# Layer 0 of a two-layer graph network: gathered sums in steps 1 to 19 of each body in place of 0 to 20

## The reference

```python
h = relu(layernorm(x));  deg = segment_sum(1, dst) + 1;  dis = rsqrt(deg)
g = (h @ W) * dis
agg = segment_sum(g[src], dst) * dis + (h @ W) * dis * dis
x = x + h + gelu(agg + b)
```

## Time and profile before

| | before |
|---|---|
| median of the runs | 3957.04 us |
| profiled execution | 3974.8 us, span 3973.0 us |
| mean granted TensorE clock | 0.769 |
| busy PE, VectorE, ScalarE, POOL | 70%, 41%, 33%, 37% of the span |
| loop of layer 0 | from 186.4 to 1191.7 us |

### The profile page before, as it was taken

The page is one execution under the profiler, slowest core; times in us unless marked ns, Lnnn a source line. Parts: engine busy times, 40 slices in busy tenths (PEclk is TensorE's granted clock), DMA queues, the critical chain, the costliest instruction groups (busy, mean ns, idle before and its releaser), DMA issues.

```text
span 3973.0 us, 102120 instructions
## 1 busy us (share of the span) xinstructions
PE 2800.8 (70%) x37635; PEld 2380.6 (60%) x37635; DVE 1621.9 (41%) x4904; ACT 1292.0 (33%) x3188; POOL 1478.0 (37%) x1462
## 2 busy tenths in 40 slices
PE   2457777677784777777777777777777777777778
PEld 2335555555563666666666666666666666666666
DVE  8735544444556333333333333333333333333333
ACT  0135555454563222222222222222222222222222
POOL 0654444333424334333333333333333333333331
PEclk6668888787886777877777777777777777777778
DMA  1000000000002122112211121221122112112211
GB/s 44 19 18 16 16 16 16 15 15 15 16 10 52 40 40 42 39 38 41 40 39 41 39 40 39 41 40 39 38 42 40 39 39 42 39 38 42 39 39 38
DMA packets 365051, 133.31 MB, mean 34 GB/s; under 512 B 312657, under 2 KB 342455, under 8 KB 364919
## 3 DMA queue, kind: packets, MB, share of 16 engines
q1 hardware_dynamic: 320248, 85.81, 9.9%
q0 software_dynamic: 44672, 45.83, 6.5%
HBM read 123.94 MB, written 7.54 MB: 33 GB/s over the span
## 4 chain that ended last, share of the span: by engine, by line
PE 67%; issue 23%; DVE 5%; another core or an unknown queue 4%; ACT 1%; DVEq 0%; POOL 0%; DMA 0%; PEldq 0%; ACTq 0%; SPq 0%; POOLq 0%
PE psum L1662 13%; PE psum L1651 12%; PE psum L1717 11%; PE psum L1519 7%; PE psum L1551 7%; PE psum L1641 7%; PE psum L1675 3%; PE psum L1699 3%; PE psum L1540 2%; PE psum L1530 1%; ACT hT L1286 1%; DVE Z L957 1%; PE psum L1485 0%; DVE work L834 0%
## 5 line engine op out<-in xcount | busy, mean ns | idle before, releaser
L673 POOL DMA_INDIRECT rows<-a_rows,idx x980 | 973.2, 993 | 1717.8 <-DMA idx<-src_by_tile 1432.9
L1651 PE MATMUL psum<-wb,eoT 128*64 128x64 f32 x6272 | 502.9, 267 | 461.4 <-issue 451.7
L1651 PEld LDWEIGHTS psum<-wb,eoT 128*64 128x64 f32 x6272 | 371.8, 170 | 571.5 <-issue 569.8
L1286 ACT ACTIVATE hT<-psum 128x392 bf16<-128x392 f32 x1152 | 518.8, 503 | 500.6 <-PE psum L1551 285.6
L1662 PE MATMUL psum<-Y,Z 128*128 128x64 bf16 x8820 | 526.4, 235 | 162.5 <-issue 162.4
L673 POOL DMA_INDIRECT rows<-g_rows,idx x416 | 411.7, 990 | 550.4 <-DMA idx<-src_by_tile 430.7
L1551 PE MATMUL psum<-Z,lo_hi 128*128 128x392 f16 x1152 | 419.5, 380 | 259.7 <-issue 169.7
L1662 PEld LDWEIGHTS psum<-Y,Z 128*128 128x128 bf16 x8820 | 465.2, 126 | 219.3 <-issue 200.2
L1519 PE MATMUL psum<-work,hT 128*128 128x192 bf16 x3528 | 513.6, 269 | 15.9 <-issue 13.2
L1356 ACT ACTIVATE Y<-psum 128x512 f16<-128x512 f32 (+1 forms) x392 | 150.0, 435 | 1151.1 <-PE psum L1699 1147.7
L1374 ACT ACTIVATE Y<-psum 128x384 bf16<-128x384 f32 (+1 forms) x588 | 255.6, 439 | 769.6 <-remote 580.9
(11 more groups left out here) (273 smaller groups left out, 2344.7 us busy)
## 6 DMA issues: line engine op xcount, KB each, us to landing
work<-in_edge_attr_dram SPq DMA_DIRECT2D x392, 128.0 KB
Z<-slot_code SPq DMA_DIRECT2D x196, 96.0 KB
rows<-a_rows,idx POOLq DMA_INDIRECT x980
rows<-g_rows,idx POOLq DMA_INDIRECT x416
idx<-src_by_tile SPq DMA_DIRECT2D x197, 2.5 KB, 1.7
wb<-b_rows SPq DMA_DIRECT2D x196, 16.0 KB
g_rows<-Y SPq DMA_DIRECT2D x1, 1600.0 KB, 7.1
a_rows<-Y SPq DMA_DIRECT2D x6, 256.0 KB, 2.3
```

The source lines that it names most:

```text
L673: pool.indirect_dma_start(out=rows[:, k, t, :], out_offset=None, in_=table, in_offset=bass.IndirectOffsetOnAxis(ap=idx[:, k, t:t + 1], axis=0)
L1286: nc.scalar.activation(counts[:, j % 2, :, t * SLOTS:(t + 1) * SLOTS], psum[:, t % 4, 0:KEYS].rearrange("p (h m) -> p h m", m=SLOTS), ACT.Copy
L1651: TT.matmul(psum[half:half + D, 2 + k % 2, t * D:(t + 1) * D], eoT[:, k % 2, t, half:half + D], wb[:, k, :], start=(t == 0), stop=False)
```

## The change

`order_of_adds` takes its places from another rule; `gathered_at` goes.

```diff
-        def gathered_at(j, steps, count):
-            q = -(-j * count // steps)
-            return q if -(-(j + 1) * count // steps) > q else None
-
         def order_of_adds(steps, count):
-            at = [gathered_at(j, steps, count) for j in range(steps)]
+            when = {1 + q * (steps - 2) // count: q for q in range(count)}
+            at = [when.get(j) for j in range(steps)]
             place_gathered, place_counted, n = [], [], 0
```

## The result

The changed kernel takes 3936.21 us (median of 20 runs, 3924.57 to 3948.18); the kernel before, in 20 runs taken with them, 3948.56 us (3932.97 to 3960.59). Forecast were 3954 us, no change, and a range of 3943 to 3973. Two things are in the miss: the 3 runs that the forecast started from had a median of 3957.04, 8.5 us above that of the 20; and the change brought 10.7 us where 2.9 were forecast.

The account below looks back on a forecast made before the run. Layer-0 gather bursts on POOL were taken to stall PE's tiles on the way to ACT for nearly their own length. Start -6.7, rows of four +3.8, rest 0: -2.9 us, from 3957.04 to 3954, range 3943 to 3973.

Parts of the forecast that it names:

- part 2: Order inside layer-0 bodies: rows of four sums cost +3.8 us, ends -4 and +7.6.
- a dearer third burst: Looped bodies: the third burst in a row of three costs 8.6 us, 1.0 more than the first two.
- Part 1: Start of body 0: step 0 without a sum, PE goes on with step 1; net -6.7 us, ends -10.2 and -3.5.
- the signs that I had named: Layer-0 start: rows wait under 2 us, first sum at 235 to 242, burst 4 alone; wrong if before 210 or after 246.
- the branch I named in one sentence: Body 0's start: PE finishes step 1 and its sum before the stall, burst 4 joins the run; gain 8.45 us.
- my sign for the looped bodies: The two looped bodies at 311 to 318 us each; wrong above 325 or below 305.
- Part 3: Last body: sums 48 to 51 in steps 1 to 4; 0 us, ends +-1.
- What a burst costs: Layer-0 gather bursts on POOL: 7.87 us each in the looped stretch, 6.5 us each in body 0.
- Rival B: Layer 0: bursts cost PE nothing, only the 10.4 us wait for first rows goes; 3946.6 us; chance 0.12.
- Rival A: Rows of four decide: each fourth burst meets the third's undrained stall; slower, 3973 to 3984 us; chance 0.17.
- Rival C: Start pays to -10.2 and rows of four cost nothing, or free steps pay -4; 3943 to 3947 us; chance 0.19.

Follow-up runs that it names:

- loops only, 5: Kernel before with the looped and last bodies as changed, body 0 as before, on chip 5: 3975.45 us, 0.9997 of the kernel before.
- start only, 5: Kernel before with only body 0's first three sums moved to steps 1, 2, 3, on chip 5: 3971.15 against 3977.15 us, 0.9990.
- body 0 only, 9: Kernel before with only body 0 as changed (rows of four from step 1), on chip 9: 3929.74 us, 0.9973 of the kernel before.
- row of 16, 5: Changed kernel with the looped bodies' sixteen sums in steps 1 to 16, on chip 5: 3963.94 us, 0.9960 of the kernel before.
- first sum in 2: Changed kernel with body 0's first sums in steps 2 to 6: chip 5 3958.36 us, 0.9947; chip 9 3924.52 us, 0.9953 of the kernel before.
- experiment 5: Kernel before with seven of eight gathers of each layer-0 burst left out: chip 9 3540.47 against 3941.30 us, 0.8982; chip 2 0.9925, also in new order.

## Why the prediction was wrong, point by point

Two terms were mis-sized. The base was 3957.04 us where 20 runs give 3948.56. And part 2, the rows of four, stood in the sum at +3.8 us and measured -1.2 (-5 to +3); its cause, a dearer third burst, came of pricing a step without a sum like one with a sum. Part 1 came near in size, but by a path that did not happen. With the measured terms the sum is 3948.6 - 8.9 - 1.2 = 3938.5; 3936.21 came, 3937.9 by the ratio.

Stretches of the layer-0 loop read from the traces (from the first tile matmul of one step to that of another), us:

| kernel, chip | steps 0 to 3 | steps 4 to 21 | sum | bodies 1, 2 |
|---|---|---|---|---|
| before | 90.4 | 237.5 | 327.9 | 629.2 |
| loops only, 5 | 93.0 | 240.1 | 333.1 | 625.0 |
| start only, 5 | 79.6 | 243.1 | 322.7 | 623.7 |
| body 0 only, 9 | 76.0 | 240.6 | 316.6 | 602.0 |
| changed | 78.6 | 240.2 | 318.8 | 605.9 |
| changed, 9 | 78.0 | 245.7 | 323.7 | 597.5 |
| row of 16, 5 | 76.6 | 249.5 | 326.1 | 609.4 |
| first sum in 2, 5 | 66.9 | 250.6 | 317.5 | 625.1 |
| first sum in 2, 9 | 65.9 | 248.0 | 313.9 | 609.8 |

**Part 1, the start: near in size by luck, wrong in the path.** Forecast -6.7 (-10.2 to -3.5). Two traces with the old start end body 0 at 330.5 on average, five with the first sum in step 1 at 321.6: -8.9, with a scatter of up to 9.5 us inside the five, four of which have the new order in body 0 too. The timed run of the start alone says -4 (-9 to +1). But I had PE caught by the stall after five or six tiles of step 1, at 0.8 us a tile, and burst 4 left alone. In fact all sixteen tiles got through at 0.4 us each before the stall began, PE waited 6.0 us for rows, and burst 4 joined the run as before (a gather every 1.25 us until 241.59). Three of the signs that I had named are answered by it: the first sum came at 204 us, before the 210 that I had called a sign of being wrong; the wait for rows was not under 2 us; and burst 4 stood behind no gap. That is the branch I named in one sentence at 8.45 us, one whole step. The step that failed is the tile's price, taken from the stretch's mean clock and not from the tiles of step 0, which stood in the earlier trace rows at 0.4 us.

**Part 2, the rows of four: wrong.** Forecast +3.8 (0 to +7.6 in its reasoning), measured -1.2 (-5 to +3). On chip 5 the looped bodies took 623.7 us in the old order and 625.0 and 625.1 in the new; on chip 9 602.0 against 597.5 and 609.8. There is no difference beyond their scatter, which also takes in my sign for the looped bodies (303 us each in the changed kernel's first trace, under the 305 that I had called wrong, and 299 to 313 in the four others with rows of four). The error can be redone from my own rows: I priced every step at 8.45 us with or without sum. With 7.21 and 1.24 (experiment 5) a pair is 40.6 - 3 x 7.21 - 2 x 1.24 = 16.5, 8.2 a burst, and a row of three 57.65 - 4 x 7.21 - 3 x 1.24 = 25.1, 8.4 a burst. The dearer third burst was the free step counted too high. The earlier trace rows gave the price of a step with a sum, and the sentence that the sum is within that figure was right; that a step without one costs the same was not looked up. The last row spoke against it: its five steps took 41.2 us, less than 5 x 8.45 = 42.25.

**Part 3, the last body: right**, 48.5 us in both traces.

**What a burst costs: right, with some luck.** 7.87 us forecast from one trace, 7.7 (7.4 to 8.0) when the gathers were taken away. With 7.21 for a step and 1.24 for a sum the same stretch gives 8.3, above the measured interval: the figure came out by the help of the wrong step price. It did not enter the difference, since the number of bursts stays. Rival B (bursts cost PE nothing) is refuted on stalling chips by experiment 5, though its 10.4 us is near the measured 10.7. The Trainium skill's sentence (SBUF — State Buffer, Who interferes with whom) that PE and ACT wait for nobody, taken as widely as the prediction took it, does not hold on the stalling chips, where ACT stands 14.90 us, and agrees with the clean ones, where leaving out seven of eight gathers moved the kernel by 0.75%. That section of the Trainium skill speaks of SBUF ports, and no run here shows whether the stalls come through these.

**Rival A** (slower by the rows of four) did not come, and the row of sixteen on chip 5, which would have made it far larger, was 16 us faster than the kernel before. **Rival C** is nearest to what came: the start near its end and the rows of four at nothing, 3943 to 3947 from a base of 3957, which is 10 to 14 under. I gave it 0.19 and the forecast 0.48; the arithmetic of part 2 took the chance from it.

**The reference of the forecast.** The range's lower end was 14 us under 3957. Three runs within 3.6 us of each other said nothing of a scatter of 28 us over 20 runs, and of medians from 3941 to 3977 between stalling chips; of the range's miss by 6.8 us this alone is more than the whole.

What stays open: on a stalling chip, how much of body 0's gain is the head start and how much the rest of its order (start only -4, -9 to +1; body 0 only -10.6, -18 to -3; the intervals overlap); and by what way the gathers delay the news of PE's tiles.

## What to carry to other kernels

Price a step with and without the part that you move before you compare patterns of it: a constant put on the wrong kind of step turns up as a pattern effect. A wait at the very start of a pipeline is worth as much work as can be done in it before the next bound closes, counted in tiles at the rate those tiles show. And a gain that rests on a stall should be read against a machine that does not have it: here the same edit is 0.3% faster or 0.2% slower by the chip.

## What the runs showed of the hardware

The same program took 3941 to 3977 us on some chips and 2174 us on others. On the first kind PE's tiles reach ScalarE late while POOL issues indirect gathers: by the records ScalarE starts on a tile up to 34.8 us after PE is done with it (tile 38 of the changed kernel, 33.4 at most in the kernel before) and stands idle for up to 14.90 us at a time in the rows above. On a clean chip (changed kernel, chip 13) it is never over 0.54 us in 1152 tiles, and so it is on the stalling chip 9 with seven of eight gathers left out. The way back from ScalarE to PE shows no such delay (0.14 or 0.15 us in the rows of the first section). The ends of matmuls are modelled in these records, but tile 39 starts at 215.46, behind tile 38 on the same engine, and even from there it is 31.6 us. On the second kind ScalarE's rows at the same place are without such gaps (changed kernel, chip 13, order of time):

```profile
186.46 12.98 ACT L1283 ACTIVATE hT<-psum 128x392 bf16<-128x392 f32 x32 [14.08 <-PE psum L1548]
207.67 2.06 ACT L1283 ACTIVATE hT<-psum 128x392 bf16<-128x392 f32 x5 [8.24 <-PE psum L1548]
210.14 5.04 ACT L1283 ACTIVATE hT<-psum 128x392 bf16<-128x392 f32 x11 [0.41 <-PE psum L1548]
```

while POOL gathers without a pause, as on the first kind in that stretch. In layer 1, with five gathers a superblock, the same instructions took 2630 to 2653 us and 1270 us from the first gather to the last, and the granted clock was 0.77 and 0.95 over the span. With seven of eight layer-0 gathers left out on a stalling chip, the loop ran almost as on a clean one with the same gathers left out (586 us on chip 9, 585 on chip 2). What makes a chip the one or the other no run here shows.
